# Attention scores issued over four row quarters of TensorE and four PSUM banks at once, in place of two turns of two

## The reference, cut to what matters

```python
# layer 2: two calls, the first over x itself (causal), the second with context as keys and values
K = jnp.einsum('bse,hed->bhsd', xk, Wk)            # 16 heads of 8
V = jnp.einsum('bse,hed->bhsd', xv, Wv)
Q = jnp.einsum('bqe,hed->bhqd', xq, Wq)
scores = jnp.einsum('bhqd,bhkd->bhqk', Q, K)
if masked:
    causal = jnp.triu(jnp.ones((xq.shape[1], sk), dtype=bool), k=1)
    scores = jnp.where(causal, -jnp.inf, scores)
att = jax.nn.softmax(scores / jnp.sqrt(sk), axis=-1)
out = jnp.einsum('bhqk,bhkd->bhqd', att, V)
# layer 3: the same form with biases, scores / sqrt(8), no mask
```

## Time and profile before

| what | value |
|---|---|
| median of 3 runs | 606.84 us (605.1 to 607.8) |
| profiled execution, its own time | 607.42 us |
| its span, first to last instruction | 605.5 us |
| TensorE matmuls busy | 420.0 us (69%) |
| VectorE busy | 461.4 us (76%) |
| ScalarE busy | 308.2 us (51%) |
| GpSimd busy | 234.4 us (39%) |
| VectorE's maxima, line 1614 | 96 of 0.689 us |
| ScalarE's exponentials, line 1153 | 96 of 0.601 us |
| chain that ended last | VectorE 43%, TensorE 39% |

### The profile page before, as it was taken

The page is one execution under the profiler, slowest core; times in us unless marked ns, Lnnn a source line. Parts: engine busy times, 40 slices in busy tenths (PEclk is TensorE's granted clock), DMA queues, the critical chain, the costliest instruction groups (busy, mean ns, idle before and its releaser), DMA issues.

```text
span 605.5 us, 11360 instructions
## 1 busy us (share of the span) xinstructions
PE 420.0 (69%) x4079; PEld 273.0 (45%) x4079; DVE 461.4 (76%) x1305; ACT 308.2 (51%) x596; POOL 234.4 (39%) x358
## 2 busy tenths in 40 slices
PE   2575341258999548103999978776589997878895
PEld 2543220135666433002556656554255664666532
DVE  5559999875667875687978888999878679796742
ACT  2476652227555323732556736762456554757641
POOL 4527775629557670631110111135355572121100
PEclk9999655559999867656999978976799998796988
DMA  7830000450000000000000000000000000000000
GB/s 222 172 32 2 1 1 0 157 122 2 2 1 1 2 0 1 1 0 1 1 2 2 2 1 2 2 2 1 1 2 1 2 0 3 1 2 2 1 17 18
DMA packets 26838, 11.86 MB, mean 20 GB/s; under 512 B 16056, under 2 KB 23712, under 8 KB 26784
## 3 DMA queue, kind: packets, MB, share of 16 engines
q1 hardware_dynamic: 26784, 11.14, 7.4%
HBM read 10.61 MB, written 0.52 MB: 18 GB/s over the span
## 4 chain that ended last, share of the span: by engine, by line
DVE 43%; PE 39%; POOL 6%; issue 6%; ACT 5%; DMA 1%; SPq 1%; DVEq 0%; ACTq 0%
PE psum L653 10%; PE psum L818 6%; DVE qs L1614 5%; PE psum L803 3%; PE psum L804 3%; PE psum L805 3%; DVE stats L1192 3%; DVE z L1200 2%; POOL work L614 2%; PE psum L990 2%; DVE at L1503 1%; DVE mv L1194 1%; PE psum L926 1%; PE psum L930 1%; DVE split L1364 1%
## 5 line engine op out<-in xcount | busy, mean ns | idle before, releaser
L536 POOL TENSOR_SCALAR vr<-mv 128x1 f32<-128x1 f32 x88 | 19.4, 220 | 217.6 <-DVE mv L1194 217.3
L614 POOL TENSOR_TENSOR work<-work 128x512 f16<-128x512 f32 x64 | 72.6, 1162 | 43.2 <-ACT work L1066 43.2
L1614 DVE TENSOR_REDUCE qs<-psum 128x4 f16<-128x512 f32 x96 | 59.6, 689 | 6.0 <-PE psum L905 5.8
L1008 ACT ACTIVATE phase<-psum 128x1024 f16<-128x1024 f16 (+1 forms) x52 | 47.5, 928 | 30.5 <-PE psum L891 15.2
L1491 DVE TENSOR_TENSOR work<-work,psum 128x512 f32<-128x512 f32 x64 | 42.9, 685 | 20.3 <-ACT work L1112 19.8
L1112 ACT ACTIVATE work<-psum 128x512 f32<-128x512 f32 x64 | 37.5, 594 | 37.2 <-PE psum L805 34.5
L1153 ACT ACTIVATE phase<-psum 128x512 f32<-128x512 f32 x96 | 49.8, 601 | 9.5 <-PE psum L930 8.8
L538 POOL TENSOR_TENSOR rstd<-vr,mhalf 128x1 f32<-128x1 f32 x88 | 50.1, 570 | 7.3
L803 PE MATMUL psum<-zTh,split 128*128 128x512 f16 x128 | 51.1, 399 | 1.9 <-DVE work L1491 1.5
L818 PE MATMUL psum<-wout,work 128*128 128x128 f16 x768 | 48.9, 223 | 3.3 <-POOL work L614 1.8
L804 PE MATMUL psum<-zTl,split 128*128 128x512 f16 x128 | 51.0, 398 | 0.0
(11 more groups left out here) (347 smaller groups left out, 1040.1 us busy)
## 6 DMA issues: line engine op xcount, KB each, us to landing
stage_f<-in_L_ffn_W_in SPq DMA_DIRECT2D x1, 2048.0 KB, 10.0
stage_f<-in_L_ffn_w SPq DMA_DIRECT2D x1, 2048.0 KB, 8.4
x<-in_x SPq DMA_DIRECT2D x1, 512.0 KB, 4.1
c<-in_ctx SPq DMA_DIRECT2D x1, 512.0 KB, 5.5
w<-in_L_ffn_W SPq DMA_DIRECT2D x2, 256.0 KB
out<-x SPq DMA_DIRECT2D x8, 64.0 KB, 1.6
rows<-in_L_xattn_b SPq DMA_DIRECT2D x4, 64.0 KB, 7.7
rows<-in_L_xattn_bo SPq DMA_DIRECT2D x3, 64.0 KB, 9.0
```

The lines of the kernel that those rows point to most:

```text
L614: ch.do(pool.tensor_tensor(hidl[:, n % 2, k, :], act[:, n % 2, k, :], hidh[:, n % 2, k, :], ALU.subtract), sem("hid_low"))
L1008: ch.do(A(out, view(u), ACT.Copy), banks.freed(stage, b, name))
L1614: ch.do(v.tensor_reduce(groups(qs[:, b, :, 3 * DA:3 * DA + 1], 4)[:, j], u, AX.X, ALU.max, negate=True), free_of(stage, b, f"s{j}"))
```

## The change

The loop over pairs of row quarters in the max stage and in the exp stage becomes one pass over all four. A unit now takes all four of its banks first, then issues the four masks (phase a), then the sixteen products with the row quarter changing fastest. The work itself, its operands, the banks and their readers stay the same; so does the order on the other engines.

```diff
                     m = stage[0]
                     banks.emptied(pe, m + "_stack", b, "qk")
-                    for pair in ((0, 1), (2, 3)):
+                    for pair in ((0, 1, 2, 3),):
                         us = {i: banks.take(pe, stage, b, f"s{i}") for i in pair}
...
                     banks.emptied(pe, m + "_again", b, "q")
-                    for pair in ((0, 1), (2, 3)):
+                    for pair in ((0, 1, 2, 3),):
                         us = {i: banks.take(pe, stage, b, f"t{i}") for i in pair}
```

## The result

| | median of its runs | ratio to before, 95% interval |
|---|---|---|
| before | 606.53 us (4 runs) | |
| changed | 612.95 us (4 runs) | 1.0098 [1.0070, 1.0127] |
| changed, a second series | 612.14 us (6 runs; before 607.18) | 1.0075 [1.0054, 1.0095] |

The account below looks back on a forecast made before the run. The prediction took TensorE to bound phase a and little elsewhere; bank waits outweighed 0.40 us saved per unit: +0.7 in phase a, +0.7 + 0.2 + 0.05 + 0.1 in b and c, sum +1.8, giving 608.6 us, range 603.5 to 612.5.

Follow-up runs that it names:

- e_mask_by_mask: Against before, phase a only: each bank taken just ahead of its own mask, masks issued singly, then all sixteen products; ratio 0.9929 [0.9912, 0.9945].

## What to carry to other kernels

Work that is issued in one piece to save a change of mode also gathers its waits; keep each wait as late as the first instruction that needs its buffer, and test the two effects apart. Here the same masks in one piece cost 2 us with the waits at their head and gained 2 with one wait ahead of each mask. Count a wait on a semaphore at what the trace shows between the end of the releaser and the start of the waiter, not at zero, and carry it along for every wait that is new on the chain.

## What the runs showed of the hardware

- From the end of a read that frees a bank to the first matmul that waited for it: 0.14 us where the waits for several banks stand ahead of that matmul (298.03 to 298.17, and 299.34 to 299.48 in before), 0.06 where each mask has the wait for its own bank alone (297.89 to 297.95 in e_mask_by_mask).
- Products of different row quarters share the array even if each quarter's four are issued behind those of the quarter before: sixteen in 0.43 us, as in 0.40 to 0.42 for the interleaved orders.
- Going from full-array masks to row-quarter products and back costs some 0.4 us for both ways: one unit with one such change took 1.36 us, with two 1.78, for the same matmuls. The Trainium skill, "TensorEngine Tiling (Array Packing)", Key Properties, says that a change of tiling mode drains the engine. The trace fits this: the first product starts 0.06 us before the last mask's recorded end, and a mask after products 0.07 before theirs (304.09 + 0.40 to 304.42 in the earlier trace rows), while of two masks in a row the second starts some 0.16 before the end of the first. Recorded ends are modelled, so this does not prove a drain.
- The same untouched matmuls took 26.6 to 31.7 us at the end of the kernel, by the low stretches of the granted clock that fell on them; the differences of 1.0 to 5.1 us are as large as what was to be measured. Phase a at a clock of 1.00 repeated to 0.02 us, so it is there that orders can be compared by one profile.
